# A recurrent layer on one Trainium2 core: three of sixteen running-sum folds move from VectorE to ScalarE

## What is computed

```python
def _L0_cond_ref(x, h0, Wx, Wh, b):
    xw = jnp.einsum('ntd,dh->nth', x, Wx) + b
    def step(prev_h, xw_t):
        next_h = jnp.tanh(prev_h @ Wh + xw_t)
        return (next_h, next_h)
    _, hs = jax.lax.scan(step, h0, jnp.swapaxes(xw, 0, 1))
    return jnp.swapaxes(hs, 0, 1)
```

## Time and profile before

| what | value |
|---|---|
| median of three runs | 7638.32 us (7632.93 to 7640.13) |
| profiled execution, its own time | 7628.87 us |
| span in its profile | 7627.0 us |
| mean granted TensorE clock | 0.935 of full speed |
| recurrent layer's loop, first to last L634 | 206.5 to 4294.9 us, 128 steps |
| busy in the stretch 203 to 4291 us | DVE 3563.5, PE 3178.4, ACT 3124.8, POOL 1032.1 us |

### The profile page before, as it was taken

The page is one execution under the profiler, slowest core; times in us unless marked ns, Lnnn a source line. Parts: engine busy times, 40 slices in busy tenths (PEclk is TensorE's granted clock), DMA queues, the critical chain, the costliest instruction groups (busy, mean ns, idle before and its releaser), DMA issues. The chain is left out here.

```text
span 7627.0 us, 150005 instructions
## 1 busy us (share of the span) xinstructions
PE 5808.2 (76%) x49401; PEld 3128.9 (41%) x49401; DVE 6085.2 (80%) x12161; ACT 4391.1 (58%) x9141; POOL 2546.8 (33%) x1905
## 2 busy tenths in 40 slices
PE   5877787778778777877787708888888887952989
PEld 3544444444444444444454303333333332531543
DVE  4988888898889888988898679999999997446333
ACT  6777787787778777877777603443444432323322
POOL 2222222222222222222222107787888874000000
PEclk9999999999999999999999959999999998986999
DMA  0000000000000000000000000000000000000000
GB/s 7 2 2 2 2 2 2 2 2 2 2 2 2 2 2 2 2 2 2 2 2 2 10 33 5 4 4 3 4 4 4 4 3 3 0 6 6 0 17 5
DMA packets 14182, 30.27 MB, mean 4 GB/s; under 512 B 3665, under 2 KB 11602, under 8 KB 12434
## 3 DMA queue, kind: packets, MB, share of 16 engines
q1 hardware_dynamic: 13586, 22.47, 1.1%
HBM read 15.12 MB, written 7.34 MB: 3 GB/s over the span
## 5 line engine op out<-in xcount | busy, mean ns | idle before, releaser
L993 POOL TENSOR_TENSOR hc<-hh,cg 128x512 f32<-128x512 f32 x1024 | 1290.3, 1266 | 350.6 <-DVE hh L975 350.2
L417 ACT ACTIVATE rx_junk<-rx_z 128x384 bf16<-128x384 f32 x2178 | 1370.2, 635 | 0.3
L915 ACT ACTIVATE ps_m<-ps_m,aneg 128x508 f32<-128x508 f32 x1024 | 673.4, 658 | 1122.2 <-DVE hh L975 1012.7
L975 DVE TENSOR_TENSOR_SCAN hh<-ps_m,bx 128x512 f32<-128x512 f32 x1024 | 1226.9, 1211 | 13.7 <-POOL bx L997 13.7
L497 POOL TENSOR_TENSOR rx_z<-rx_z 128x512 f32<-128x512 f32 x256 | 384.6, 1502 | 2332.8 <-ACT rh_z L433 2329.5
L630 DVE TENSOR_REDUCE rh_ends<-rh_z 128x4 f32<-128x1536 f32 x512 | 960.1, 1917 | 132.9 <-ACT rh_z L433 132.9
L879 PE MATMUL ps_m<-hc,pick 128*128 128x512 f32 x2048 | 1057.7, 600 | 8.0 <-POOL hc L993 6.8
L333 PE MATMUL r_ps<-rx_z,negid 128*128 128x256 f32 x2192 | 553.4, 398 | 277.9 <-POOL xsl L540 184.0
L503 POOL TENSOR_TENSOR rx_z<-rx_z 128x1024 f32<-128x1024 f32 x274 | 656.2, 2395 | 73.4 <-DVE rx_z L596 36.7
L954 DVE TENSOR_TENSOR bx<-ps_m,bg 128x512 f32<-128x512 f32 x896 | 595.7, 671 | 90.0 <-PE ps_m L895 89.5
L309 PE MATMUL r_ps<-rh_z,negid 128*128 128x256 f32 x2048 | 496.8, 385 | 166.1 <-ACT r_ps L428 164.8
(11 more groups left out here) (401 smaller groups left out, 10792.0 us busy)
## 6 DMA issues: line engine op xcount, KB each, us to landing
rows_scratch<-pc SPq DMA_DIRECT2D x48, 128.0 KB
rows<-rows_scratch SPq DMA_DIRECT2D x128, 48.0 KB
ew<-in_e SPq DMA_DIRECT2D x3, 1024.0 KB, 7.0
rh_z<-in_x_dn SPq DMA_DIRECT2D x1, 1024.0 KB, 4.7
xcur<-in_x_dn SPq DMA_DIRECT2D x1, 1024.0 KB
out_x<-xcur SPq DMA_DIRECT2D x1, 1024.0 KB, 3.9
qi<-in_f_q SPq DMA_DIRECT2D x1, 384.0 KB, 3.2
xpw<-in_xp_t SPq DMA_DIRECT2D x1, 257.0 KB
```

What stands on the lines that cost most here:

```text
L417: e.activation(junk[:, n % JUNK], xz[i][:, :, n, 2:K2].rearrange("p c k -> p k c"), ACT.Copy, accum_out=xsum[:, i, n:n + 1]).then_inc(x_fo ...
L915: e.activation(da[un % NDA][:, :, 1:T], ps[:, un % 2, :].rearrange("p (n t) -> p n t", n=NG4)[:, :, 1:T], ACT.Exp, scale=aneg[:, 0:1]).the ...
L975: e.tensor_tensor_scan(hh[un % NBUF][:], da[un % NDA].rearrange("p n t -> p (n t)"), bx[un % NBUF][:], 0.0, ALU.mult, ALU.add).then_inc(sc ...
L993: e.tensor_tensor(hc[un % NHC][:], hh[un % NBUF][:], cg[:], ALU.mult).then_inc(weighted, 1)
```

## The change

ScalarE, after its copies of all four quarters of the remainder, folds the sequences 13, 14 and 15 of the h chain as three ACTIVATEs with an accumulator output, in the way of the x chain's folds. Ahead of them it waits for its own last copy. VectorE's fourth quarter shrinks from four sequences to one, and VectorE waits for the three columns before `pre`. A scrap tile and a semaphore (`tail`) are added.

```diff
+        TAIL = 3
+        rjunk = sb("rh_junk", [128, TAIL, D, 3], BF16)
...
                     for c in range(2, NRC):
                         rest(c)
+                    e.wait_ge(ra, KA * t + A_REST[NRC - 1])
+                    for i_ in range(TAIL):
+                        n = N - TAIL + i_
+                        e.activation(rjunk[:, i_], hz[:, :, n, 2:K2].rearrange("p c k -> p k c"), ACT.Copy,
+                                     accum_out=ends[:, n:n + 1]).then_inc(tail, 1)
                     x_fold(g - 1, other, SECOND, THIRD)
                     e.wait_ge(v, KV * t + V0 + VGUESS)
...
                     for c in range(NRC):
                         e.wait_ge(ra, KA * t + A_REST[c])
-                        j = tl.inc(e.tensor_reduce(ends[:, quarter(c)], fold(hz, quarter(c)), mybir.AxisListType.XY, ALU.add))
+                        n = slice(quarter(c).start, min(quarter(c).stop, N - TAIL))
+                        j = tl.inc(e.tensor_reduce(ends[:, n], fold(hz, n), mybir.AxisListType.XY, ALU.add))
                     tl.wait(j)
+                    e.wait_ge(tail, TAIL * t + TAIL)
```

More of the change, by code:

```diff
@@ L106, in rnn @@
             "x_copied", "x_summed", "x_evened", "x_negdiff", "x_rest", "x_folded", "x_biased"))
-        xt_mm, xw_cp, stp, stl, tri = (sem(x) for x in ("xt_mm", "xw_cp", "stp", "stl", "tri"))
+        xt_mm, xw_cp, stp, stl, tri, tail = (sem(x) for x in ("xt_mm", "xw_cp", "stp", "stl", "tri", "tail"))
         KD = 8
```

## The result

| | before | with the change |
|---|---|---|
| median | 7635.62 us (7632.39 to 7640.13, 4 runs) | 7693.61 us (7691.72 to 7698.54, 4 runs) |
| ratio, 95% interval | | 1.0077 [1.0059, 1.0094] |
| span of the profiled execution, mean granted clock | 7627.0 us, 0.935 | 7692.2 us, 0.924 |

The change is slower by 58 us, and the forecast was 7693. In the step of rows 3 that point is 2038.22 + 1.08 = 2039.30; in the step shown here it is 1897.33. Lines have moved: the new folds are L476, an x fold L419, `pre` L643, `x_copy` L407, `x_rest_copy` L411, the copy of the h product L457, the unread matmuls L349.

The account below looks back on a forecast made before the run. It took the order of waits as the bound, neither engine being saturated: VectorE's fold on the path, ScalarE's `x_copy` 1.33 us behind. Odd and ordinary steps +35, clock +20, so +55 on 7638.32 gave 7693 us, range 7645 to 7750.

Parts of the forecast that it names:

- ScalarE: ScalarE's queue: a 0.14 us wait and three folds of 0.63 each; x folds 2.03 later, `x_copy` ends 1.31 later.
- the whole 1.23 us are taken up by the wait for `x_copy`: Ordinary steps: `pre` and first diagonal come 1.23 us earlier, but the h product waits for `x_copy`, leaving 0.02 gained.
- a sign named as wrong: Start of the h product: still being released by VectorE, not by `x_copy`, would show the prediction wrong.
- Ordinary steps: The 96 steps with s = 0 to 5: 0.02 us shorter each, -2 us in all, plus 3 us for the clock.
- s = 6: 16 steps where `xsp` hangs on the folds: 0.52 us longer each, plus 0.65 each for the clock.
- s = 7: 16 steps where `xsl` waits behind `x_bias` and the folds: 1.79 us longer each, plus 0.4 for the clock.
- Faster: Rival: VectorE is the bound and ScalarE's folds are covered, 1.23 us gained in 112 steps; 7529 us, chance 0.09.
- No change: Rival: L347's matmuls in one piece keep the clock up and give back 50 of 55 us; 7643 us, chance 0.11.
- Slower still: Rival: the h product runs at 1.2 GHz in nearly every ordinary step, +115 us; 7753 us, chance 0.16.

Follow-up runs that it names:

- e2: The change, but VectorE folds all sixteen sequences again and ScalarE's three folds go to a tile nobody reads; 7693.84 us, ratio 1.0070 to the kernel before.
- e3: The change with GpSimd's second subtraction cut to one column for each sequence, leaving out part of the x remainder; 7680.70 us, ratio 1.0052 to the kernel before.
- e1: The change without ScalarE's three folds and VectorE's wait for them, so three sums are left out; 7644.51 us, ratio 1.0005 to the kernel before.
- e6: The kernel before with GpSimd's sums released by VectorE's scan instead of ScalarE's copies, 0.7 us earlier; 7646.95 us, ratio 1.0019.
- e8: The change with two folds on ScalarE instead of three, and GpSimd's sums released earlier, by VectorE's scan; 7638.59 us, ratio 1.0012 to the kernel before.
- e4: e1 with GpSimd's second subtraction cut to one column for each sequence; 7420.13 us, ratio 0.9711 to the kernel before.
- e7: The change with one fold on ScalarE instead of three, and GpSimd's sums released earlier, by VectorE's scan; 7647.12 us, ratio 1.0023 to the kernel before.
- e10: e7 with ten unread matmuls instead of six ahead of the h product, the first issued earlier; 7565.21 us, ratio 0.9903 to the kernel before.

## Why the prediction was right in its time, and where it was wrong

- **ScalarE: right.** The first new fold starts 0.04 behind its own copy (0.03 forecast), three take 1.89, L480 starts 6.95 after rest instead of 5.15 (1.79 later forecast), `x_copy` ends 1.25 later (1.31 forecast). e2, with these three and VectorE's wait for them alone, has the whole cost.
- **The step that failed: "the whole 1.23 us are taken up by the wait for `x_copy`".** They were never won. I took `pre` to start 1.23 earlier, which it does, and to last 0.39 as in the earlier trace rows. That length was not the operation's own: `cl`, of the same size, takes 0.17 right behind it, and without the subtraction beside it `pre` takes 0.176 (e3). The 0.39 was the last of a hold by GpSimd, whose row at that point (2040.62) the working did not use. The time came out the same since `x_copy`, the second limit, stood at nearly the same place: 14.46 after rest, with the first diagonal at 14.41. In e3, where the hold is taken away, the failed step is what happens, in the 32 steps that `x_copy` releases.
- **What released the product: a sign named as wrong came.** In the 34 ordinary steps at full clock the product starts 0.13 behind the diagonal, as before, so VectorE still releases it. It starts 0.10 behind `x_copy`, which lets it start after 0.06 in e3: the limit left out of the working is about 0.05 us the later one. That it is not later by more is luck. In 56 of the 62 steps below full clock the product follows the unread matmuls without a gap.
- The Trainium skill, SBUF — State Buffer, section SBUF: two separate sides, says that a VectorE operation with two SBUF inputs and a GpSimd operation that reads SBUF exclude each other for the whole instruction, whichever starts first. The traces agree: `pre` (two inputs) ends 0.03 to 0.04 behind the subtraction in before, the change and e1, while the reductions (one input) overlap L504 and the start of L510 and neither waits for the other's end. By that rule and GpSimd's row, `pre` would have ended at 3.72 in the working too.
- **Ordinary steps: right by two errors.** +1 us was forecast (-2, and 3 for the clock), +3.7 measured. Steps of both kinds got shorter by 0.17, which is 16 us in 96 steps; 15 more of them were below full clock, at 1.32 each, which gives 20 back. The forecast had neither; that they cancel is luck. Of the 0.17, 0.10 is not in the fold. VectorE's long scan of tanh started 0.13 behind the operation ahead of it before, and 0.03 with the change (rows below, the scan is L213 and then L215). The instruction between the two is another one in the built program: before, it waits for VectorE's own result, and with the change for ScalarE's operands, which have been ready for long.

```profile
2048.98 0.40 DVE L210 TENSOR_TENSOR t<-rh_z 128x176 f32<-128x176 f32 x1
2049.51 1.26 DVE L213 TENSOR_TENSOR_SCAN to<-t 128x528 f32<-128x528 f32 x1
...
1906.99 0.40 DVE L212 TENSOR_TENSOR t<-rh_z 128x176 f32<-128x176 f32 x1
1907.42 1.26 DVE L215 TENSOR_TENSOR_SCAN to<-t 128x528 f32<-128x528 f32 x1
```

- **s = 6: too small.** 0.52 and 0.65 for the clock were forecast, 1.42 measured. The clock's part is in the rows: after an idle 2.59, L271 runs at 0.67 and takes 2.08 instead of 1.48, 0.60 more; then the unread matmuls, 2.11, keep TensorE 1975.05 - 1974.60 = 0.45 beyond the end of `x_copy` instead of 0.13, 0.32 more. 0.52 + 0.60 + 0.32 = 1.44. The h product itself was hardly slowed there: 1.69 on average from its start to its copy, 1.64 before.
- **s = 7: right.** TensorE's wait rose by 13.29 - 11.50 = 1.79, the step by 1.88 inside a turn (2.19 forecast). Of the 0.4 that was put down for the clock, 0.09 is left, and no row had shown it. At the end of a turn it rose by 2.23, but that step is 47.92 in e1 too, where no fold is late, so its share is open.
- **The rivals.** Faster needed ScalarE's folds to be hidden; e2 shows that they are not. No change needed the clock to pay; it charged instead. Slower still, the lower clock in nearly every ordinary step, did not come with the change (62 of 96), but it did in e6 to e8 (82 to 88), where TensorE's idle stretch grew. The Trainium skill, in TensorE: Matmul & The Clock Gate, section HAM oscillation, describes a wait that lowers the clock in each turn of a loop. The traces of e6 to e8 agree in that nearly every turn has it, but TensorE's waits are 2.3 to 2.8 us on average here, shorter than in the loop of that section. Nor does the length of the wait say it alone: in e3 it is longest, 3.1 us, with 55 such steps.

## What to carry to other kernels

A short operation that takes longer than its equals can be held and not slow, as `pre` was: look at what the other engines do at the moment it ends, before counting on its start. Where an engine is relieved, list every limit behind the first and test them in pairs, as here e1, e3 and e4: each limit removed alone gave little or nothing, both gave 3%. And before trimming the steady step, look at the odd ones: two copies of 0.5 us at another place in GpSimd's queue were worth 2%.

## What was not expected of the hardware

- The hold between VectorE and GpSimd works both ways. In e7 GpSimd's `x_bias`, 128x16, took 1.13 us instead of the 0.22 it takes in e1: it ends at 1898.15, when VectorE's scan L215 ends (1896.88 + 1.26 = 1898.14).
- Four additional matmuls that nobody reads, the first of them issued earlier, took the ratio from 1.0023 to 0.9903 (e7 to e10), about 90 us; ending TensorE's work 0.7 us sooner without them made it slower, 1.0019 [1.0010, 1.0028] (e6), though `pre` ended 0.2 sooner.
- Unread matmuls at the lower clock can hold the work that they are there for: in the step shown they end 0.64 us behind `x_copy`, and the product starts as they end. No run changed them with three folds on ScalarE, so what they cost there is not shown.
